# Placing the maxima of the next phase among an attention kernel's key tiles by elapsed time, with the differences' scores directly behind the value products

## What is computed

```python
scores = jnp.einsum('bhqd,bhkd->bhqk', q, k) / jnp.sqrt(jnp.float32(DH))
attn = jax.nn.softmax(scores, axis=-1)          # layers 0, 1, 3
...
scores = jax.nn.sigmoid(jnp.einsum('blhd,bshd->bhls', q, k))   # layer 2
...
x = x + _L0_xattn_ref(_layernorm(x, axis=-1), ctx_1024, ctx_1024, ...)
x = x + _L0_ffn_ref(_layernorm(x, axis=-1), ...)
```

## Time and profile before

| | |
|---|---|
| median of 3 runs | 4546.94 us (4540.88 to 4552.91) |
| profiled execution | 4547.49 us |
| its span | 4545.1 us |
| PE, ACT, DVE busy | 84%, 86%, 63% |
| granted clock, mean | 0.964 |

### The profile page before, as it was taken

How to read it: one execution, slowest core, us unless ns; L and a number is a source line. 1 busy time by engine, 2 the same in 40 slices (tenths; PEclk the granted TensorE clock), 3 DMA queues, 4 the chain that set the end, 5 groups by cost and what they waited for, 6 DMA issues and landing times.

```text
span 4545.1 us, 69698 instructions
## 1 busy us (share of the span) xinstructions
PE 3840.0 (84%) x26742; PEld 873.8 (19%) x26742; DVE 2873.7 (63%) x5732; ACT 3898.4 (86%) x4328; POOL 831.1 (18%) x719
## 2 busy tenths in 40 slices
PE   5888888888889888898888999888788888888886
PEld 2121111111121211122112222111111111122112
DVE  2978888778886788867612432110685678877823
ACT  3588998899988889888899899988987889888993
POOL 4010000430025300152522111111001110034002
PEclk8699999999999999999999999999998989999998
DMA  4221000100021110110102221110001000011001
GB/s 123 75 57 36 12 14 17 45 15 12 14 57 38 33 33 14 36 39 28 39 14 58 68 64 37 35 41 21 14 25 32 27 10 14 12 39 30 5 1 50
DMA packets 124482, 151.31 MB, mean 33 GB/s; under 512 B 29272, under 2 KB 76384, under 8 KB 124080
## 3 DMA queue, kind: packets, MB, share of 16 engines
q1 hardware_dynamic: 122640, 145.53, 11.8%
q10 hardware_dynamic: 1504, 1.28, 0.2%
HBM read 123.21 MB, written 23.51 MB: 32 GB/s over the span
## 4 chain that ended last, share of the span: by engine, by line
PE 49%; ACT 24%; DVE 16%; issue 6%; DMA 1%; SPq 0%; POOL 0%; POOLq 0%; ACTq 0%; DVEq 0%
PE av L860 19%; ACT prob L1019 14%; DVE mpart L1130 10%; PE scores L850 7%; PE side L881 6%; ACT above L1027 6%; DVE above L1134 4%; PE scores L958 4%; PE side L976 4%; PE side L958 2%; ACT ag L1070 1%; PE scores L872 1%; ACT tx L1061 1%; PE side L850 1%; PE scores L1000 1%
## 5 line engine op out<-in xcount | busy, mean ns | idle before, releaser
L1019 ACT ACTIVATE prob<-scores 128x1024 f32<-128x1024 f32 x2998 | 2939.4, 1036 | 225.8 <-PE scores L850 196.8
L1130 DVE TENSOR_REDUCE mpart<-side 128x1 f32<-128x512 f32 (+1 forms) x3456 | 2124.4, 656 | 681.5 <-PE side L881 670.6
L860 PE MATMUL av<-prob,VA 128*9 128x512 f32 x6528 | 869.6, 605 | 40.3 <-ACT prob L1019 37.3
L860 PE MATMUL av<-prob,VB 128*9 128x512 f32 x6528 | 868.7, 605 | 18.6 <-ACT prob L1019 17.9
L850 PE MATMUL scores<-QP,KA 32*128 32x512 f16 x2996 | 565.4, 393 | 175.4 <-ACT above L1027 120.1
L850 PE MATMUL scores<-QP,KB 32*128 32x512 f16 x3000 | 554.7, 386 | 163.6 <-ACT above L1027 93.7
L881 PE MATMUL side<-KA,QP 32*128 32x512 f16 (+1 forms) x2112 | 623.7, 391 | 41.3 <-DVE mpart L1130 21.2
L881 PE MATMUL side<-KB,QP 32*128 32x512 f16 (+1 forms) x2112 | 582.2, 382 | 43.5 <-DVE mpart L1130 29.0
L1134 DVE CUSTOM_DVE_ANT_0 above<-side,above 128x512 f32<-128x512 f32 x768 | 513.9, 685 | 73.1 <-PE side L881 66.0
L1027 ACT ACTIVATE above<-scores 128x1024 f32<-128x1024 f32 x384 | 393.2, 1024 | 175.6 <-PE scores L872 114.3
L1019 ACT ACTIVATE prob<-side 128x1024 f32<-128x1024 f32 x266 | 288.8, 1086 | 24.0 <-PE scores L850 23.6
(11 more groups left out here) (190 smaller groups left out, 2749.7 us busy)
## 6 DMA issues: line engine op xcount, KB each, us to landing
cwb<-weights SPq DMA_DIRECT2D x80, 256.0 KB, 4.0
KA<-kstacks SPq DMA_DIRECT2D x384, 48.0 KB
KB<-kstacks SPq DMA_DIRECT2D x384, 48.0 KB
Fin<-in_Fin SPq DMA_DIRECT2D x64, 256.0 KB, 2.8
kstacks<-hi SPq DMA_DIRECT2D x112, 128.0 KB, 2.4
ctxc<-in_ctxT SPq DMA_DIRECT2D x36, 256.0 KB, 3.1
kstacks<-lo SPq DMA_DIRECT2D x56, 128.0 KB, 2.6
hT<-in_mask SPq DMA_DIRECT2D x16, 400.2 KB, 3.3
```

The lines of the kernel that those rows point to most:

```text
L860: last = pe.matmul(AV[ROWS * h:ROWS * h + VC, :], V[l % 2][:, kt, g * HG + h, :], prob[:, (e + h // 2) % RING, (h % 2) * QB:(h % 2) * QB + ...
L1019: act.activation(prob[:, e % RING, :], pair.rearrange("p a b -> p (a b)"), ACT.Exp if softmax(l) else ACT.Sigmoid, scale=SCALE).then_inc(s ...
L1130: dve.tensor_reduce(part, bank, AX.X, ALU.max).then_inc(sem["red"], 1)
```

## The change

Only the order of steps changes. The share that `find` is held to goes by `gone[t]`, an estimate of elapsed time: each tile counts 1.95 plus its ACT background or 1.8 plus its PE background, whichever is more, and 0.97 more behind a difference. The maxima may be spread until `END` = 3 steps before the window's end, not 8, and the differences over `e - 20 - a`. In a tile whose step 3 will emit a difference (`due`) step 2 emits one item, not two, and step 3 none, so that the difference follows `av` directly. In the tile behind it (`late`) step 0 emits up to three items and step 2 one, unless that tile has a long PE background step.

```diff
@@ -467,11 +467,15 @@
 COST = dict(red=0.62, both=0.7, resid=0.7, sum=0.7, sumsq=0.7, yadd=0.7, norm=0.35, rden=0.3, finc=0.7, fina=0.3, finb=0.2, routea=0.3, routeb=0.4,
             routee=1.0, routef=0.5, routeg=0.5, routeh=0.5, routej=0.5, routek=0.5, routel=0.5, routec=1.0, routed=0.4, gatea=0.7, gateb=0.7,
             ysum=0.7, upc=0.7)
+
+COST_ACT = dict(tanh=0.6, ac=0.6, gc=0.6, yc=0.6, upc=0.6, gelu=3.2, kc=0.7, vc=0.6, qsplit=1.5, xTc=0.6, oflipc=0.6, cwTc=0.6, rexp=0.2, drain=0.6)
+COST_PE = dict(up=1.08, down=1.08, kv=1.08, qproj=1.08)
+TILE_ACT, TILE_PE, RELU = 1.95, 1.8, 0.97
 Q = 4 * KT
 
 PACE = {3: (1.3, True), 4: (1.5, True)}
 
-LEAD = 12
+LEAD, END = 12, 3
 
 
 def attention_steps(units):
@@ -511,9 +515,29 @@
 
         return max(first * Q, (p - 1) * Q - LEAD), p * Q - LEAD
 
+    tile_act, tile_pe = {}, {}
+    for at, s in back:
+        if s.eng == "ACT":
+            tile_act[at // 4] = tile_act.get(at // 4, 0.0) + COST_ACT[s.what]
+        elif s.eng == "PE":
+            tile_pe[at // 4] = tile_pe.get(at // 4, 0.0) + COST_PE.get(s.what, 0.4)
+
+    def elapsed(a, e, ahead):
+
+
+        now, out, behind = 0.0, {}, {(at + 4) // 4 for at, d in ahead}
+        for t in range(a, e):
+            by_act, by_pe = TILE_ACT + tile_act.get(t // 4, 0.0), TILE_PE + tile_pe.get(t // 4, 0.0)
+            now += max(by_act, by_pe) / 4
+            if t % 4 == 0 and t // 4 in behind:
+                now += max(by_act + RELU, by_pe + 0.35) - max(by_act, by_pe)
+            out[t] = now
+        return {t: x / now for t, x in out.items()}
+
     out = []
     n = 0
     p = first + 1
+    late = False
     spent, single, both, ready, ahead, total = 0.0, [], [], [], [], None
 
     def find(half, t, most):
@@ -521,7 +545,7 @@
         nonlocal spent
         a, e = window(p)
         for _ in range(most):
-            if t < e - 8 and spent >= total * (t + 1 - a) / (e - 8 - a):
+            if t < e - END and spent >= total * gone[t]:
                 return
             if both[half] and (ready[half][0] <= t if ready[half] else False):
                 i = both[half].pop(0)
@@ -548,24 +572,30 @@
             spent, single = 0.0, [list(range(0, half_of)), list(range(half_of, FIRST_BOTH))]
             both = [[i for i in range(FIRST_BOTH, len(ITEMS)) if ITEMS[i][2] // 2 == half] for half in range(2)]
             ready = [[], []]
-            ahead = [(a + (e - 24 - a) * d // len(DIFS), d) for d in range(len(DIFS))]
+            ahead = [(a + (e - 20 - a) * d // len(DIFS), d) for d in range(len(DIFS))]
+            gone = elapsed(a, e - END, ahead)
             total = FIRST_BOTH * COST["red"] + (len(ITEMS) - FIRST_BOTH) * COST["both"]
-            total += sum(COST.get(s.what, 0.15) for at, s in back if s.eng == "DVE" and a <= at < e - 8)
+            total += sum(COST.get(s.what, 0.15) for at, s in back if s.eng == "DVE" and a <= at < e - END)
         if q in (0, 2):
             half = q // 2
             for i in ((), (0, 1))[q == 0] if wide(t // Q, kt) else (half,):
                 out.append(Step("PE", "score", (t // Q, kt, i)))
                 out.append(Step("ACT", "exp", (t // Q, kt, i)))
-            if has:
-                find(1 - half, t, 2 if t < window(p)[1] - 8 else 5)
+            due = has and ahead and ahead[0][0] <= t - q + 3 and not ready[0] and not ready[1]
+            if has and t >= window(p)[1] - END:
+                find(1 - half, t, 5)
+            elif has:
+                late = late and tile_pe.get(t // 4, 0.0) < 1.0
+                find(1 - half, t, (1 if due or late else 2) if half else 3 if late else 2)
         if q == 3:
             if kt:
                 out.append(Step("PE", "av", (t // Q, kt - 1)))
             elif t // Q > first:
                 out.append(Step("PE", "av", (t // Q - 1, KT - 1)))
-            if has:
+            late = has and ahead and ahead[0][0] <= t and not ready[0] and not ready[1]
+            if has and not late:
                 find(0 if len(single[0] + both[0]) > len(single[1] + both[1]) else 1, t, 1)
-            if has and ahead and ahead[0][0] <= t and not ready[0] and not ready[1]:
+            if late:
                 d = ahead.pop(0)[1]
                 out.append(Step("PE", "dif", (p, d)))
                 out.append(Step("ACT", "relu", (p, d)))
```

## The result

The changed kernel takes 4584.36 us, median of six runs, against 4546.31 before: a ratio of 1.0083, 95% interval 1.0070 to 1.0096. It is slower by 38 us where 90 us less were forecast. The profiled execution has a span of 4577.5 us (4545.1 before).

A forecast was written before the change was run, and what follows sets the result against it. ACT and PE were each busy some 85%, with DVE almost without room in light phases. Gains of 48 us in light and 42 in mixed phases, together 90, took 4547 to 4457 us; range 4395 to 4538.

The forecast's parts named there:

- The relu's wait: At a difference: the relu starts 0.48 us earlier; gain 3.4 us a light phase and 40 us in the mixed ones.
- the first sign of being right: Over the whole kernel: idle before relus falls from 175.6 us to under 110.
- Part (2): Spread by elapsed time: 2.6 us back in each light phase, net 2 us for all fifteen mixed phases.
- part (1): Order around a difference: the difference directly behind av, gaining 3.4 us a light phase and 40 us in mixed phases.
- Four-maxima tiles become rare: Light phases: 3.1 maxima a tile and 4.7 behind a difference, where every tile had 3.7.
- The check "from the other side": Light phases can't be shorter than DVE's 107.8 us plus 1.4 of tail plus 0.3 at each difference: 114; forecast 118.
- the third maximum behind the score: Tile behind a difference: it repeats a row group for 0.27 us, inside PE's 1.06 us of idle, so counted as nothing.
- Pace and end: New spread of maxima and later window end: 2.6 us a light phase, net 2 us for the mixed ones.
- The loss in heavy tiles: Mixed phases: a little more PE work in some 540 heavy tiles, 8 us lost, 29 at worst.
- The later end: At a phase's turn: DVE's 2.80 us of idle falls to about 1; a possible 14 us exposure was taken as 0.
- The slower one: Rival, behind a difference: the third maximum waits for its bank and delays av and exponentials; 4583 us, chance 0.13.
- DVE as the new bound: Rival: DVE can't take reductions faster, so the relu gain returns as holds before av; 4537 us, chance 0.13.

The follow-up runs named there:

- e14: The kernel of e12 with step 3's item put behind the difference, so that the difference follows av directly: 4476.46 us, ratio 0.9849.
- e12: The kernel of e2, but step 3 takes heads 0 and 1 only where more than eight more of their items are left: 4469.40 us, ratio 0.9838.
- e9: Changed kernel with plain reductions reading half their chunk and products between av and the next first score on row groups 2 and 3: 4408.32 us, ratio 0.9699.
- e2: Kernel before with the new pace, later end and new times of the differences, but the old positions: 4481.04 us, ratio 0.9864.
- e10: Changed kernel with up to two items again behind the second score in a difference's tile: 4544.32 us, ratio 0.9993.
- e13: The kernel of e12 without step 3's item in a difference's tile, and up to three items behind the next first score: 4535.03 us, ratio 0.9979.
- e5: Changed kernel, same order of steps, with products between av and the next first score always on row groups 2 and 3: 4553.42 us, ratio 1.0013.
- e11: Kernel before with maxima spread until three steps before the window's end and differences over e - 20 - a: 4512.24 us, ratio 0.9931.
- e6: Kernel before, same order of steps, with products between av and the next first score always on row groups 0 and 1: 4578.79 us, ratio 1.0066.

## Why the prediction was wrong, point by point

- **The relu's wait, right.** "The relu would wait 0.05 or less" where nothing holds av, about half of it won: 98.6 us went, where 27 + 40 were forecast (43 in the light phases, 55 in the mixed). The mechanism is as described and the size was low. So the first sign of being right, idle before relus under 110, came true in a kernel that is slower: it says nothing of the gain.
- **What the gain is worth, the first step that failed.** The sum booked each us of idle taken from before a relu as a us of span. The runs show it come back before exponentials: +122.4 against -98.6 in the changed kernel, +18.5 against -17.8 in e14, which differs from e12 in the place of the difference. In a light phase, where DVE is busy for 107 of 124 us, a relu that starts earlier only moves ACT's wait to the next exponentials, unless DVE gets its work in time. With cheap reductions and without the row groups the change does gain: 33 us (e9).
- **The number of maxima by tile, the step that gave the wrong sign.** Part (2) took 3.1 maxima for every tile and 4.7 behind a difference. The limits of part (1) (one behind the second score, none at step 3) let only 2.2 into the difference's tile; the pace then makes up for it: 4.7 in the next tile, as said, and 3.7 in the one after, not 3.1. "Four-maxima tiles become rare" is true of e2, not of the change. The text had both limits in it and did not add them up. The two tiles behind a difference went from 1.93 and 2.06 us to 2.25 and 2.33. Half a maximum put back into the difference's tile is worth 41 us (e10), and one taken out of a good order costs 64 (e13). Before, too, the count is not even: 3.9, 3.6 and 3.3, not 3.7 in every tile.
- **DVE's idle at a difference.** "0.3 idle at each difference" was a guess below the 0.47 of the earlier trace rows; the trace has 0.44 and 0.82 around one difference. The check "from the other side" rested on it and gave 114, which allows DVE 6.2 us of idle in a light phase; it has 20.2.
- **Whose row groups, overlooked.** The text weighed the row groups of the third maximum behind the score, where PE waits anyway, and took the step 3 item as it was. But step 3 picks the pair of heads with more items left, and three items for heads 2 and 3 against one for heads 0 and 1 tips that choice from 11 to 513 items of heads 0 and 1. Price by e5: 32 us. The Trainium skill ("TensorE: Matmul & The Clock Gate", Part 3) says that weight loads overlap running matmuls only where row groups differ. The trace agrees in the effect and not in the letter: the second product's weights are recorded at 1083.58, beside the running maximum of its group, and it is the product that starts 0.22 later, at 1083.79. The row that the prediction read for it was another thing: at 526.63 the second of the two maxima waited for DVE to give a bank back, as the prediction itself says earlier, so its 0.27 us is no price of a repeated group.
- **Pace and end, right in sign, far too small.** 21 us in the light phases and 2 in the mixed were forecast for them; e2 gives 62, of them 40 in the light phases (991.7 to 951.1) and 23 in the mixed. The loss in heavy tiles that the text allowed for (8 us, and 29 at worst) was not seen.
- **The later end, right.** DVE's idle at a light phase's turn fell from 2.80 to 1.16 us, where about 1 was forecast, and the fear for the next phase's first score (14 us) has no sign in e11, which is faster.
- **The rivals.** The slower one named 4583 and 4584 was measured, which is luck: its mechanism is at most half of it. It let the third maximum wait for a bank behind the difference. There DVE was dry; the banks are full one tile later, where av goes late. The range, 4395 to 4538, left that rival out at a chance of 0.13. What was given no term at all is the row groups of step 3 and the second tile behind a difference. "DVE as the new bound" was right for the limit, wrong in assuming that the limit only takes a gain away; an uneven supply makes it cost more than before.

## What to carry to other kernels

Where two engines are both nearly full, a wait removed on one is worth only what the other can follow: ask what the slow consumer gets to do in the stretch that was shortened. Before counting an edit to limits, write the number of items in each slot for one whole period, and whose they are. A choice by "which side has more left" passes a change in one slot on to all others.

## What the runs showed of the hardware

Two products of 32 rows in different row groups start together (0.39 us for the pair); behind one in the same group the second starts 0.22 later and the pair takes 0.60 (1083.57 and 1083.79). With 513 such neighbours in front of scores that came to 32 us, 0.06 each, and with 1001 in the old order to 30, 0.03 each. In part this is because fewer of them delay anything: the second product of a first score starts 0.19 us or more late 417 times in the changed kernel and 616 times in e6. For these it is 0.08 and 0.05 each, and the rest of the difference was not settled. It was also not settled why the later end alone helps the mixed phases and hardly the light ones.
